# One GpSimd order, one copy on ScalarE, the offsets at the step's end, and gated values in PSUM

## The reference

```python
def step(prev_h, xw_t):
    next_h = jnp.tanh(xw_t + prev_h @ Wh)
    return (next_h, next_h)
...
hg = xn @ W1 + b1
a, gate = jnp.split(hg, 2, -1)
return a * jax.nn.gelu(gate, approximate=False) @ W2 + b2
```

## Time and profile before

| | us |
|---|---|
| median of 3 runs | 3302.94 (3302.47 to 3304.96) |
| the profiled execution | 3300.16 |
| its span | 3298.3 |
| PE busy | 2684.7 (81%) |
| DVE busy | 2738.2 (83%) |
| ACT busy | 2025.1 (61%) |
| POOL busy | 2484.4 (75%) |

### The profile page before, as it was taken

The page is one execution under the profiler, slowest core; times in us unless marked ns, Lnnn a source line. Parts: engine busy times, 40 slices in busy tenths (PEclk is TensorE's granted clock), DMA queues, the critical chain, the costliest instruction groups (busy, mean ns, idle before and its releaser), DMA issues.

```text
span 3298.3 us, 52212 instructions
## 1 busy us (share of the span) xinstructions
PE 2684.7 (81%) x12585; PEld 1645.0 (50%) x12585; DVE 2738.2 (83%) x7678; ACT 2025.1 (61%) x3842; POOL 2484.4 (75%) x2673
## 2 busy tenths in 40 slices
PE   4777777777777777777777779879999999999997
PEld 2333333333333333333333337746777777777776
DVE  4999999999999999999999984367877778777774
ACT  3666666666666666666666653356666666667665
POOL 6888888888888888888888870068778777787783
PEclk9999999999999999999999999879999999999998
DMA  5333333333333333333333341000010101010000
GB/s 131 70 71 70 71 70 72 69 75 66 75 67 76 64 77 66 75 68 73 70 71 71 70 96 36 1 1 1 0 37 0 37 0 37 0 37 0 0 0 7
DMA packets 368022, 163.09 MB, mean 49 GB/s; under 512 B 285166, under 2 KB 298228, under 8 KB 367220
## 3 DMA queue, kind: packets, MB, share of 16 engines
q1 hardware_dynamic: 367988, 162.65, 23.5%
HBM read 156.81 MB, written 5.80 MB: 49 GB/s over the span
## 4 chain that ended last, share of the span: by engine, by line
POOL 32%; DVE 26%; issue 19%; PE 18%; ACT 3%; POOLq 1%; DVEq 1%; DMA 0%; SPq 0%; ACTq 0%
POOL diag_h L637 8%; POOL qkv_w L643 5%; POOL qkv_w L630 5%; POOL kT L623 4%; DVE bank L1052 3%; DVE rot_s L1269 3%; DVE rot_c L1269 3%; DVE ss L1272 3%; POOL qT L623 3%; POOL qkv_w L632 3%; PE bank L1595 3%; PE bank L1673 2%; PE bank L1647 2%; PE bank L1455 2%; DVE mx L1184 2%
## 5 line engine op out<-in xcount | busy, mean ns | idle before, releaser
L1356 PE MATMUL bank<-diag_h,w_part 128*128 128x512 f32 x1024 | 339.5, 457 | 233.3 <-POOL diag_h L637 123.6
L630 POOL TENSOR_TENSOR qkv_w<-b,offset 128x512 f32<-128x512 f32 x258 | 269.5, 1044 | 298.5 <-ACT b L765 288.2
L1052 DVE TENSOR_REDUCE qkv_w<-qkv_w 128x4 f32<-128x1536 f32 x256 | 448.3, 1751 | 47.4 <-ACT qkv_w L778 32.9
L1052 DVE TENSOR_REDUCE bank<-qkv_w 128x2 f32<-128x768 f32 x512 | 455.4, 953 | 5.5 <-ACT qkv_w L785 4.9
L1371 PE MATMUL bank<-qT,wh 128*128 128x256 f32 (+1 forms) x768 | 278.4, 482 | 207.6 <-DVE qT L1034 178.0
L710 POOL TENSOR_TENSOR qk<-rot_c,rot_s 128x512 f32<-128x512 f32 x192 | 257.0, 1339 | 207.7 <-DVE rot_s L1269 207.7
L778 ACT COPY qkv_w<-bank 128x512 f32<-128x512 f32 x258 | 221.5, 859 | 289.7 <-PE bank L1356 289.7
L1356 PEld LDWEIGHTS bank<-diag_h,w_part 128*128 128x128 f32 x1024 | 184.0, 203 | 426.6 <-DVE bank L1047 233.3
L1356 PE MATMUL bank<-diag_x,w_part 128*128 128x512 f32 x1032 | 388.1, 498 | 9.0 <-DMA diag_x<-diag_ring 9.0
L637 POOL TENSOR_TENSOR diag_h<-eye,part 128x512 fp32r<-128x512 f32 x384 | 394.7, 1043 | 0.0
L785 ACT COPY qkv_w<-bank 128x256 f32<-128x256 f32 x512 | 217.3, 506 | 208.4 <-PE bank L1356 208.4
(11 more groups left out here) (235 smaller groups left out, 6397.9 us busy)
## 6 DMA issues: line engine op xcount, KB each, us to landing
diag_x<-diag_ring SPq DMA_DIRECT2D x259, 512.0 KB, 6.1
qkv_w<-in_L_ffn_Wqkv SPq DMA_DIRECT2D x6, 1536.0 KB
diag_ring<-X SPq DMA_DIRECT2D x264, 4.0 KB, 5.4
diag_ring<-o_fin SPq DMA_DIRECT2D x8, 512.0 KB, 8.3
o_w<-in_L_ffn_Wo SPq DMA_DIRECT2D x6, 512.0 KB
w<-in_L_ffn_W SPq DMA_DIRECT2D x6, 341.0 KB
b<-in_L_ffn_b SPq DMA_DIRECT2D x6, 341.0 KB
w<-in_L_ffn_W SPq DMA_DIRECT2D x6, 128.0 KB
```

Of the source, the lines that this page charges most:

```text
L630: pool.tensor_tensor(adds[1][:, rows, :, 1], src, offset[:, 0:1].unsqueeze(2).to_broadcast([P, 4, D]), ALU.add)
L1052: return dve.tensor_reduce((pre, bias_at[0])[n][:, a:b], chain[n][:, a:b, :], AX_X, ALU.add)
L1356: return pe.matmul(dst, w_part[:, n, w], diag[n][:, d, a:b, :].rearrange("p n k -> p (n k)"), start=False, stop=True, skip_group_check=True)
```

## The change

- `minus_h` on POOL is made for half 0 only, and comes behind the third diagonal and the copy to hT. Minus the guess of half 1 is made by ACT (`place_minus_h`) out of PSUM bank 1, as 12 minus the sum, between the rests of half 0 and those of half 1; it waits for DVE's difference of half 1. There are two semaphores for it now, one a half.
- POOL makes x's triangles for step t+2 ahead of `place_sums_x`, each behind a new wait for PE's sums of x of the same half, which read the triangle before.
- PE writes the offsets behind x's rests, at the end of the step, and waits for ACT's new copy.
- The value of the feed-forward stays in PSUM bank 6; the product reads it there, and `attention_out`, which writes bank 6, waits for the product.

```diff
--- before.py
+++ after.py
@@ -215,7 +215,6 @@
         xnT = sb("xnT", [D, T])
         gate_in = sb("gate_in", [P, FI])
         gate_g = sb("gate_g", [P, FI])
-        val = sb("val", [P, FI])
         hg = sb("hg", [P, FI])
         hgT = sb("hgT", [P, 3, T])
         o_fin = sb("o_fin", [P, NB, D])
@@ -305,7 +304,7 @@
         split_h = sem("split_h")
         x_split = sem("x_split")
         guess_placed = sem("guess_placed_h")
-        minus_placed = sem("minus_placed_h")
+        minus_placed = [sem("minus_placed_h%d" % half) for half in range(2)]
         diag_upper_h = sem("diag_upper_h")
         diag_lower_h = [sem("diag_lower_h%d" % half) for half in range(2)]
         diag_x_ready = [sem("diag_x%d" % half) for half in range(2)]
@@ -637,11 +636,10 @@
                 pool.tensor_tensor(diag[n][:, d, rows, :], eye[:].unsqueeze(1).to_broadcast([P, 4, D]),
                                    values.unsqueeze(2).to_broadcast([P, 4, D]), ALU.mult).then_inc(done, 1)
 
-            def minus_h(half, count):
-                rows = slice(4 * half, 4 * half + 4)
+            def minus_h(count):
                 pool.wait_ge(guess_placed, count)
-                pool.tensor_tensor(adds[0][:, rows, 0:D - 1, 2], adds[0][:, rows, 0:D - 1, 1],
-                                   signs[:, 1:2].unsqueeze(2).to_broadcast([P, 4, D - 1]), ALU.mult).then_inc(minus_placed, 1)
+                pool.tensor_tensor(adds[0][:, 0:4, 0:D - 1, 2], adds[0][:, 0:4, 0:D - 1, 1],
+                                   signs[:, 1:2].unsqueeze(2).to_broadcast([P, 4, D - 1]), ALU.mult).then_inc(minus_placed[0], 1)
 
             def at_step(m):
                 return xT[:, bass.ds(m, 1), :].rearrange("p a n -> p (a n)")
@@ -663,16 +661,16 @@
                 pool.wait_ge(split_h, this)
                 diagonal(0, 0, 0, part[:, 0, 0:4], diag_upper_h)
                 diagonal(0, 1, 0, part[:, 1, 0:4], diag_lower_h[0])
-                minus_h(0, counts[0])
                 diagonal(0, 0, 1, part[:, 0, 4:8], diag_upper_h)
                 pool.tensor_copy(hT[:, bass.ds(t, 1), :].rearrange("p a n -> p (a n)"), h_now[:]).then_inc(h_ready, 1)
-                minus_h(1, counts[1])
-
+                minus_h(counts[0])
+                later = at_step(value(pool, t + 2))
+                for half in range(2):
+                    pool.wait_ge(sum_ready[1], counts[2 + half])
+                    triangle(1, later, half, tri_x)
                 pool.wait_ge(x_scanned, this)
                 place_sums_x(0, counts[2])
                 place_sums_x(1, counts[3])
-                for half in range(2):
-                    triangle(1, at_step(value(pool, t + 2)), half, tri_x)
             pool.wait_ge(h_static, T + 1)
             pool.tensor_copy(hT[:, T, :], h_now[:]).then_inc(h_ready, 1)
 
@@ -772,6 +770,13 @@
                 act.wait_ge(sum_ready[0], count)
                 act.activation(adds[0][:, 4 * half:4 * half + 4, :, 1], bank[:, half, :].rearrange("p (n k) -> p n k", k=D),
                                ACT.Identity, bias=offset[:, 0:1], scale=1.0).then_inc(guess_placed, 1)
+
+            def place_minus_h(count):
+
+                act.wait_ge(diff_ready, count)
+                act.activation(adds[0][:, 4:8, 0:D - 1, 2],
+                               bank[:, 1, :].rearrange("p (n k) -> p n k", k=D)[:, :, 0:D - 1], ACT.Identity,
+                               bias=offset[:, 1:2], scale=-1.0).then_inc(minus_placed[1], 1)
 
             def place_rests_x(half, count):
                 act.wait_ge(rest_ready[1], count)
@@ -804,6 +809,7 @@
                 act.wait_ge(split_h, this)
                 lower_h()
                 place_rests_h(0, counts[0])
+                place_minus_h(counts[1])
                 place_rests_h(1, counts[1])
                 act.wait_ge(sum_placed[1], counts[1])
                 act.wait_ge(rest_placed[1], counts[1])
@@ -1158,7 +1164,7 @@
                     def placed_h(m):
                         dve.wait_ge(rest_placed[0], quarters[m])
                         if m % 2 == 0:
-                            dve.wait_ge(minus_placed, counts[m // 2])
+                            dve.wait_ge(minus_placed[m // 2], this)
 
                     placed_x(counts[0])
                     n_x = step(fold(1, 0, 4))
@@ -1305,11 +1311,11 @@
                     dve.wait_ge(hg_ready, count)
                     dve.tensor_tensor(gate_in[:], bank[:, 7, 0:FI], bias[:, FI:2 * FI], ALU.add).then_inc(gate_ready, 1)
                     dve.wait_ge(hg_ready, count + 1)
-                    dve.tensor_tensor(val[:], bank[:, 6, 0:FI], bias[:, 0:FI], ALU.add).then_inc(val_ready, 1)
+                    dve.tensor_tensor(bank[:, 6, 0:FI], bank[:, 6, 0:FI], bias[:, 0:FI], ALU.add).then_inc(val_ready, 1)
                 if old:
                     dve.wait_ge(val_ready, i - 2)
                     dve.wait_ge(gelu_ready, i - 2)
-                    dve.tensor_tensor(hg[:], val[:], gate_g[:], ALU.mult).then_inc(mul_ready, 1)
+                    dve.tensor_tensor(hg[:], bank[:, 6, 0:FI], gate_g[:], ALU.mult).then_inc(mul_ready, 1)
                 if mid:
                     mine = xm[:, par, :]
                     dve.wait_ge(o_ready, i - 1)
@@ -1421,10 +1427,10 @@
                 for half in range(2):
                     pe.wait_ge(rest_placed[0], quarters[half])
                     sums_x(half, counts[2 + half])
-                pe.wait_ge(guess_placed, counts[1])
-                offset_h()
                 for half in range(2):
                     rests_x(half, counts[2 + half], landed)
+                pe.wait_ge(minus_placed[1], this)
+                offset_h()
 
             def transposed(dst, src, cols, n, done):
 
@@ -1668,7 +1674,7 @@
                     wo_j = o_w[:, bass.ds(place(pe, i - 2)[2], 1)]
                     pe.wait_ge(attT_copied, two - 2)
                     if old:
-                        pe.wait_ge(val_ready, i - 2)
+                        pe.wait_ge(mul_ready, i - 2)
                     for m in range(8):
                         ins = pe.matmul(bank[:, 6, 0:D], attT[:, m, :], wo_j[:, :, m, :].rearrange("p a n -> p (a n)"),
                                         start=(m == 0), stop=(m == 7))
```

## The result

The changed kernel is **slower**: 3383.5 us against 3304.0 before (medians of four runs each), ratio 1.0239 (95% interval 1.0218 to 1.0260). The forecast was 3276 us, faster, with a range up to 3328. The profiled execution took 3388.9 us, with a span of 3387.1.

The account below looks back on a forecast made before the run. VectorE (DVE) was taken as the recurrence's floor, with POOL making some steps late. Late steps -55, clock falls +40, feed-forward -12 sum to -27 us, giving 3276 us from a median of 3302.9; range 3234 to 3328.

Parts of the forecast that it names:

- The gain from the late steps: Recurrence: POOL's new order ends steps where h's second triangle comes late; 0.44 us a step over 126 steps, 55 us.
- any delay of POOL in mid-step makes the next step late: Recurrence: POOL ends x's triangles at 14.94 us and is wanted at 15.01, so it has no slack.
- The check by the waits: Recurrence: DVE's 56.4 us of waits for ACT's guess, less 0.17 in a good step, gives nearly the same gain.
- The cost of the falls: Recurrence: drops of PE's clock to half rate move onto h's sums, where DVE waits for them; +40 us.
- as many as now, some 46: Recurrence: the number of clock falls expected on h's sums, each priced at 0.87 us.
- My upper bound of 68 x 1.3: Recurrence: clock falls on h's sums in more than every second step, 1.3 us each, 88 us.
- 2.6 us of idle or light work ahead of the sums: Recurrence: PE's stretch at each step's end without full matmuls after the change, where it was 1.8 us.
- Rival 2: Recurrence: clock falls hit h's sums in more than half of the steps; +21 us, 3324 us; chance 0.30.
- the times within a step: Recurrence: second x triangle from 8.9 us, POOL's sums to 14.0, ACT's copy 0.95, x's rests to 12.7.
- Rival 3: Recurrence: POOL stays late waiting for PE's second x sums, only the feed-forward gain remains; 3291 us; chance 0.15.
- the feed-forward part: Feed-forward stage: product reading the value from PSUM falls from 1.30 to 0.52 us; 0.26 us in 44 units, 12 us.

Follow-up runs that it names:

- e9: Kernel before with the value in PSUM and two unused full PE matmuls a step (between h's sums and rests, behind x's rests): 3237.8 us, ratio 0.9788.
- e3: Changed kernel plus two unused float32 128x512 PE matmuls at the step's end, just before the offsets: 3238.4 us, ratio 0.9784.
- e10: Changed kernel plus one unused float32 128x512 PE matmul ahead of the offsets at the step's end: 3250.1 us, ratio 0.9826.
- e4: Kernel before with only the offsets moved behind x's rests: 3304.3 us, ratio 1.0001.
- e8: Kernel before plus one unused float32 128x512 PE matmul between h's sums and h's rests: 3294.9 us, ratio 0.9971.
- e2: Changed kernel with the offsets put back ahead of x's rests: 3275.6 us, ratio 0.9901.
- e7: Kernel before with only POOL's new order; no copy on ACT, offsets in mid-step, value in SBUF: 3350.9 us, ratio 1.0137.
- e6: Changed kernel with the light offset matmuls written four times over at the step's end: 3403.2 us, ratio 1.0295.
- e11: Kernel before with the value in PSUM and one unused full PE matmul behind x's rests: 3263.7 us, ratio 0.9892.
- e1: Kernel before with only the feed-forward value kept in PSUM: 3292.7 us, ratio 0.9957.

## Why the prediction was wrong

- **The gain from the late steps: right in size, wrong in cause.** 55 us were to be had, and e9 and e3 have them (steps of 14.52 and 14.50 against the 14.51 worked out). But the step "any delay of POOL in mid-step makes the next step late" stopped one question short: what delays it. It was the fall of the clock in mid-step. I had written of these falls that DVE hardly waits for them; they cost 1.2 us each ((14.95 - 14.51) x 126 = 55 us, less 2 us for the two on the sums, over 46), and 0.98 of that one step later, by way of POOL: a late step takes 15.49 us on average. POOL's order was only what passed the delay on. The check by the waits does not come out: 56.4 us less 0.17 in each of 119 steps is 36, and e9, without a late step, still has 16.4 us of that wait in the same window. So 40 of the 55 us lay in it, not nearly all.
- **The cost of the falls: the mechanism right, the term mis-sized.** The falls moved onto h's sums, as forecast. I took "as many as now, some 46" at 0.87 us, 40 us. That is the step that failed: it was 114 at (15.74 - 14.51) x 126 / 114 = 1.36 us, **155 us**, so the sum is -55 + 155 - 11 = +89 us by the trace, not -27. The number 46 had nothing to stand on: it came from a loop in which every second or third step was stretched by its fall and PE's work with it. Behind such a step PE stood idle ahead of the next sums for 0.8 us on average, behind the others for 1.8. With falls on the sums PE is still done early: in the changed kernel the mean is 2.4 us behind a step with a fall and 2.2 behind one without, so every step meets the same idle time, and the light offsets on top. My upper bound of 68 x 1.3 took the price about right and the number at little over half. The price goes by where in the step the fall begins. 72 of the 114 (63%) begin earlier than 1.5 us into it, ahead of both samples of the earlier trace rows, and these steps take 16.17 us on average, 1.66 over 14.51; the other 42 take 15.38, and those 0.87 over it are the forecast's price.
- **What the number goes with.** I had worked out 2.6 us of idle or light work ahead of the sums, 1.8 before, and still took the number as it was. Over the kernels that ran, the mean time from the end of PE's last full matmul to h's first sum (the offsets counted as nothing) puts the falls on the sums in order: 1.4 us in the kernel before (2 falls), 1.9 in e10 (18), 2.0 in e4 (29), 2.1 in e8 (44), 2.3 in e2 (46), 2.7 in e7 (86), 2.9 in the changed kernel (114), 3.0 in e6 (116), and none in e3 and e9 with 1.0. Where the falls lie also shifts that time, so the order is no proof of a cause; e3, which changes nothing but this stretch, is the test of it.
- **Rival 2** had the sign and the place, not the size: 3324, measured 3383. It got 0.30, and that was too little, since both samples in the trace spoke for it.
- **The offsets' move** I counted with the rest. e2 shows that on top of the other parts it decides: with it 114 falls, without it 46. That e2 took 3275.6 us, the forecast's time, is chance: it is another kernel than the one forecast. e7 and e4 show that neither POOL's order nor the offsets' move needs the other to put falls on the sums: 86 and 29.
- **Right**: the times within a step. POOL's second x triangle from 9.00 (8.9 forecast), its last sum to 14.05 (14.0), ACT's copy of 0.96 us (0.95) inside its idle time, x's rests to 12.6 (12.7). Rival 3 is out: POOL was never late.
- **Right**: the feed-forward part, 12 us; 14 measured alone (interval 9 to 20), 11 by the trace of the changed kernel. Of VectorE's 0.79 us a unit 0.3 came through, about POOL's share, as worked out (0.26 x 44 is 11.4 us, not 12).

What stays open: why one program runs in one pattern or the other (e4: 3294 to 3323 us), and what starts the falls after 50 quiet steps in e10 and e11. The runs show that it happens, not what sets it.

## What to carry to other kernels

In a loop where PE is not the bound, look at where in the step the granted clock falls and who waits then, before moving work: freeing another engine can end PE's work sooner and bring the fall onto the path. A wait that comes and goes from step to step with the same code is a sign of it; match the late steps with the falls of the step before. Where PE has idle time ahead of a matmul that all wait for, full matmuls with no use for their result are worth a try: here two of them a step took the kernel before from 3292.7 (e1) to 3237.8 us (e9), 1.7%, more than any of the reordering (e2, with the value in PSUM too: 3275.6).

## What the hardware showed that I had not expected

- Light matmuls did not hold the clock here: with four times the offset matmuls (one row of weights, bf16) PE was busy for 87% of the stretch and the clock 0.87; with two float32 128x512 matmuls in the same place (e3) PE was busy for 85% and the clock 1.00.
- In the changed kernel PE was never idle for more than 2.7 us at a stretch in a step, and the clock fell nearly once a step all the same, for 3.41 or 6.83 us. In e6, with 116 falls, it was never idle for more than 1.4 us.
- VectorE's product with both inputs in SBUF took 1.30 us beside a POOL instruction and 0.515 with one input in PSUM, and POOL's product (L710, then L708) fell from 1.54 to 1.29 us at the most. That agrees with the Trainium skill, "SBUF — State Buffer", section "SBUF: two separate sides", by which a VectorE instruction with two SBUF inputs and a GpSimd instruction that reads SBUF take a shared pair of ports in turn.
- The Trainium skill, "TensorE: Matmul & The Clock Gate", section "What's actually happening", says that the clock is throttled by default and that activity releases it. e3 agrees in kind: with two more full matmuls a step the clock was 1.00, where it was 0.87 without them. The same section puts the penalty of a ramp under 1% of a typical span. That figure was no guide to this loop, in which the clock falls anew in nearly every step: the time beyond the floor was 155 of 3387 us, 4.6%, where the prediction had at most 33 us by it.
